# Middle layer norm of five chunks without a second transposition: centred B and a product on GpSimd with spread deviations

## The chip, the cores and the metric

One core of one Trainium2 chip runs the kernel. The metric is device time in microseconds, the median of three runs of the kernel before: 383.70 us (383.51 to 383.71). TensorE runs the matmuls and the transposes (PE in the profile, with its weight loads as PEld), VectorE (DVE) and ScalarE (ACT) work between them, GpSimd (POOL) does elementwise work in SBUF, and SyncE (SP) issues transfers.

## What is computed

The reference is a block of feed-forward, recurrent layer, feed-forward on an input of 8 sequences, 512 positions and 128 features, in float32:

```python
x = x + 0.5 * ffn(layernorm(x))      # ffn: silu(x W1) * (x W2), two gelu layers of 512, back to 128
z = layernorm(x)                     # the middle norm
xB = z @ B                           # B is 128 x 16
h_t = tanh(xB_t + h_(t-1) @ A.T)     # scan over 512 positions
x = x + (h @ C) @ W_out.T + b_out
x = x + 0.5 * ffn(layernorm(x))
```

layernorm takes mean and variance over the 128 features, without weights. Only `z @ B` is needed of the middle norm.

## The kernel before

The 4096 tokens are cut into 8 chunks of 512. The feed-forward network runs on one chunk after the other, 16 turns in all (8 chunks, two networks), with features on the partitions and 512 tokens along the free axis. Each large matmul is done twice, with a high and a low float32r part of its input (`y_hi`, `y_lo`), accumulated in one PSUM bank. ScalarE computes the activations and their rounded high parts; VectorE and GpSimd subtract to get the low parts. Each engine has its own hand-written order, and they meet only through semaphores that count up.

A turn g on TensorE is: layer 2 of chunk g (four output tiles m, four inputs k), with layer 4 of chunk g - 1 inside it, then layer 1 of chunk g + 1, layer 3 of chunk g. Turns 1 to 5 are `early_turn`; turns 3 to 5 also carry eight steps of the scan, and turns 4 and 5 are a hardware loop. In turn g the middle norm of chunk g - 1 (`mid`) is made. Its steps in the kernel before are:

- VectorE's `layer4` writes the chunk's residual stream to `x1c`; SP saves it.
- `middle_tokens` transposes `x1c` on TensorE, four 128 x 128 blocks into the bank `MI`: tokens on the partitions.
- `middle_stats` takes mean and variance on VectorE (`mv_m`), and `inverse_std("m", ...)` on GpSimd makes `rs_m`, the inverse deviations (128 x 4: token on the partition, block along the free axis).
- `normalise("m", ...)` on VectorE, four instructions, writes the normed tokens to `xnt_m`.
- `to_features("m", ...)` transposes them back on TensorE, four more blocks, line L316 of the profile.
- `middle_copy` on ScalarE copies them from `MI` to `xn2`.
- `x_times_b`, the last of TensorE's turn, multiplies `xn2` with `b_rep` (B twice over) into the bank `SC`, and `keep_xb` on ScalarE saves the result.

The first norm of the chunks 3 to 7 is done in another way already: GpSimd's `spread_std` writes mean and inverse deviation to `mr`, SP writes them to DRAM (`mr_row`) and reads them back as one row broadcast to all partitions (`mr_rep`, in the freed part of `w_raw`), and GpSimd's `spread_normalise` subtracts and multiplies, tokens along the free axis.

GpSimd's order in an early turn is: `spread_std`, `inverse_std("m")`, then `rest` (y2_lo of k = 0 and 2, y1_lo of k = 0 of the next chunk, y3_lo of k = 0, y1_lo of k = 1 and 2), then `spread_normalise`. The line L1507 is y1_lo, L1513 y2_lo or y3_lo. VectorE does the others: y2_lo and y3_lo on L853 and y1_lo of k = 3 on L848, behind the cast `y1_high` on L840. SP's loop over k = 0 to 4 is: `save_x1`, the write of `mr_row` (L1643), and its broadcast (L1646).

The scan's matrices are split and masked by `mix_parts` and `mix` on VectorE (L895, L899, L906). They stand in the turns that carry no scan step, which are the turns 1 and 2; both turns run them whole.

Of the kernel before, what the change touches and what calls it, by code (L numbers as in the profile page):

```python
# [48 lines left out]
WARM = 19  # L49
TURNED = 3  # L50
# [10 lines left out]
def build(nc, xT, xtok, w1T, w2T, h1T, h2T, w3T, scales, Ablk, Brep, CTrep, WoutT, ident_d, mask_d, outT):  # L61
    with ExitStack() as ctx:
# [52 lines left out]
        b_rep = sb("b_rep", [P, 2 * STATES])  # L115
        ct = sb("ct", [P, P])
# [106 lines left out]
        x1_saved = sem("x1_saved")  # L223
        xn2_r = sem("xn2_r")
# [42 lines left out]
        def through_t(kind, g):  # L267

            return turned(g) if kind == "f" else g
# [13 lines left out]
        def _(pe):  # L283
# [146 lines left out]
            def x_times_b(c):  # L430
                pe.wait_ge(xn2_r, c + 1)
                wait(pe, step_h, (c - SKIP) * CSTEPS)

                for j in range(2 * HALVES):
                    half = j % HALVES
                    mm = nc.tensor.matmul(SC[j * 2 * STATES:(j + 1) * 2 * STATES, 0:HCOLS], b_rep[:, :],  # L436
                                          xn2[:, half * HCOLS:(half + 1) * HCOLS], start=True, stop=True)
                mm.then_inc(xb_mm, 1)

# [22 lines left out]
            def early_turn(g, gen, mid, scan):  # L462
# [14 lines left out]
                layer2(g, 1, gen)  # L477
                middle_tokens(mid, 0)
# [8 lines left out]
                to_features("m", xnt_m, MI, mid)  # L487
# [9 lines left out]
                if isinstance(mid, int) and mid == 0:  # L497
                    pe.wait_ge(ld_scan, 48)
                x_times_b(mid)
# [273 lines left out]
        def _(dve):  # L773
# [34 lines left out]
            def normalise(kind, g, bankt, mv, rs, out):  # L808
                dve.wait_ge(rstd[kind], g + 1)
                wait(dve, feat[kind], through_t(kind, g))  # L810
                for q in range(QT):
# [43 lines left out]
            def layer4(phase, g, c):  # L855
                dve.wait_ge(l4_mm, g + 1)
                if phase == 0:
                    dve.wait_ge(ld_xall, 16)
                    wait(dve, x1_saved, 16 * g)
                    wait(dve, tok["m"], g)  # L860
                    res, dst = cols(x_all, c), x1c[:, :]
# [27 lines left out]
            def mix_parts(i):  # L889

                if i == 0:
# [4 lines left out]
                    return  # L896
                dve.wait_ge(ld_scan, 48)
# [31 lines left out]
            def early_turn(g, mid, scan):  # L929
                def step(t):  # L930
                    if scan is not None and t is not None:
                        scan_low(scan, t)
                    if scan is None and t in (0, 1):
                        mix_parts(t)
                    if scan is None and t == 6:
                        mix(0)
                    if scan is None and t == 7:
                        mix(1)
                        mix(2)
# [9 lines left out]
                normalise("m", mid, MI, mv_m, rs_m, xnt_m)  # L949
# [251 lines left out]
        def _(act):  # L1201
# [44 lines left out]
            def middle_copy(c):  # L1246
                act.wait_ge(feat["m"], c + 1)
# [28 lines left out]
            def early_turn(g, mid, scan):  # L1276
# [17 lines left out]
                middle_copy(mid)  # L1294
# [201 lines left out]
        def _(pool):  # L1496
            def inverse_std(kind, g, mv, ve, rs):
# [3 lines left out]
                wait(pool, normed[kind], through_t(kind, g))  # L1501
# [38 lines left out]
            def early_turn(g, mid):  # L1540
                spread_std(g + 2)
                inverse_std("m", mid, mv_m, ve_m, rs_m)
                rest(g, True)
# [14 lines left out]
            def rest(g, nxt):  # L1558
                low(g, 0, y2_hi_r, 2, y23, y2_hi, y2_lo, y2_lo_pool, (l3_mm, 4 * g))
                low(g, 2, y2_hi_r, 2, y23, y2_hi, y2_lo, y2_lo_pool, (l3_mm, 4 * g))  # L1560
# [162 lines left out]
```

## Time and profile before

| | |
|---|---|
| median of the runs | 383.70 us |
| the profiled execution: its time / its span | 383.75 us / 381.8 us |
| TensorE busy | 374.3 us, 98% of the span |
| VectorE / ScalarE / GpSimd busy | 74% / 68% / 47% |
| chain that ended last, TensorE's share | 92% |

The busy time of an engine says how full it is on the average, not which wait ends last. The chain follows the work back from the last instruction, each time to what released it. A timeline gives start, duration, engine, line, operation, output and inputs of each instruction, and in square brackets the idle time before it with the event that ended it. Starts are in microseconds from the span's start.

### The profile page before, as it was taken

The numbers are of one execution on the slowest core, as the hardware profiler recorded it, in microseconds if no ns is written. First come the engines' busy times: TensorE is split into PE (matmuls) and PEld (weight loads), VectorE is DVE, ScalarE is ACT, GpSimd is POOL, SyncE is SP. The second block draws the span as 40 slices with busy tenths as digits, with TensorE's granted clock in tenths as the row PEclk, the third lists the DMA queues.
The fourth block names the chain that finished last, engine by engine and source line by source line (L and its number), as shares of the span: only waits on it lengthen the run. The fifth ranks groups of instructions, "written<-read, shape, count | busy, mean of one in ns | idle before, by whom it ended". The sixth has DMA issues, their size and how long they took to land.

```text
span 381.8 us, 6521 instructions
## 1 busy us (share of the span) xinstructions
PE 374.3 (98%) x1773; PEld 297.2 (78%) x1773; DVE 283.3 (74%) x719; ACT 261.4 (68%) x605; POOL 177.8 (47%) x161
## 2 busy tenths in 40 slices
PE   7999999999999999999999999999999999999995
PEld 6877776867878787878778788888888788887774
DVE  5977989797797877677868866767867677686713
ACT  3889585676858678676685767858576875857654
POOL 2645264685646658342551623535324352533421
PEclk9999999999999999999999999999999999999999
DMA  7920010202001020000001000010100101010000
GB/s 225 433 116 1 28 57 15 70 2 83 3 29 55 2 83 0 27 1 29 28 2 55 3 28 27 2 55 2 56 0 15 40 0 55 0 40 17 2 28 32
DMA packets 7805, 16.64 MB, mean 44 GB/s; under 512 B 1888, under 2 KB 2912, under 8 KB 7520
## 3 DMA queue, kind: packets, MB, share of 16 engines
q1 hardware_dynamic: 6768, 16.01, 11.1%
q10 hardware_dynamic: 1008, 0.29, 0.3%
q8 instruction: 12, 0.20, 0.2%
q14 instruction: 17, 0.14, 0.1%
HBM read 9.99 MB, written 2.12 MB: 32 GB/s over the span
## 4 chain that ended last, share of the span: by engine, by line
PE 92%; DVE 4%; ACT 2%; issue 1%; DVEq 0%; ACTq 0%
PE F L288 71%; PE FR L288 8%; PE SC L504 2%; DVE y_lo L853 1%; PE FR L316 1%; PE F L541 1%; PE F L532 1%; ACT y_hi L1236 1%; DVE cw_mix L906 1%; PE MI L296 1%; PE MI L316 1%; PE FR L306 1%; PE SC L288 1%; PE SC L436 1%; PE F L534 1%
## 5 line engine op out<-in xcount | busy, mean ns | idle before, releaser
L288 PE MATMUL F<-y_hi,w_hi 128*128 128x512 f32 (+1 forms) x484 | 197.2, 408 | 0.9 <-DVE y_lo L853 0.6
L288 PE MATMUL F<-y_lo,w_hi 128*128 128x512 f32 (+1 forms) x484 | 188.4, 390 | 0.0
L288 PEld LDWEIGHTS F<-y_hi,w_hi 128*128 128x128 f32 x484 | 90.9, 188 | 25.4 <-issue 6.8
L1233 ACT ACTIVATE y<-F,sc 128x512 f32<-128x512 f32 x111 | 76.1, 686 | 43.5 <-PE F L288 42.3
L288 PEld LDWEIGHTS F<-y_lo,w_hi 128*128 128x128 f32 x484 | 91.2, 188 | 15.3
L1507 POOL TENSOR_TENSOR y_lo<-y,y_hi 128x512 fp32r<-128x512 f32 x48 | 66.7, 1396 | 59.0 <-DVE y_hi L840 48.1
L853 DVE TENSOR_TENSOR y_lo<-y,y_hi 128x512 fp32r<-128x512 f32 x79 | 64.9, 822 | 38.7 <-ACT y_hi L1236 38.7
L1513 POOL TENSOR_TENSOR y_lo<-y,y_hi 128x512 fp32r<-128x512 f32 x48 | 62.6, 1311 | 35.4 <-ACT y_hi L1236 35.4
L1236 ACT ACTIVATE y_hi<-F,sc 128x512 fp32r<-128x512 f32 x111 | 76.1, 685 | 0.0
L1252 ACT ACTIVATE h<-SC 128x32 fp32r<-128x32 f32 x96 | 18.8, 196 | 49.3 <-PE SC L451 48.3
L288 PE MATMUL F<-xn_hi,w_hi 128*128 128x512 f32 x118 | 49.4, 418 | 0.0
L823 DVE SCALAR_TENSOR_TENSOR u<-th,F 128x512 f32<-128x512 f32 x61 | 41.5, 680 | 8.1 <-ACT th L1215 8.0
L288 PE MATMUL F<-xn_lo,w_hi 128*128 128x512 f32 x118 | 46.2, 392 | 0.0
L833 DVE SCALAR_TENSOR_TENSOR y<-F,s12h,u 128x512 f32<-128x512 f32 x58 | 43.3, 747 | 1.6
L1215 ACT ACTIVATE th<-F,s1h 128x512 f32<-128x512 f32 x61 | 41.3, 689 | 2.5 <-PE F L288 2.5
L872 DVE TENSOR_TENSOR h<-SC,h 64x32 fp32r<-64x32 f32 x96 | 17.1, 178 | 18.3 <-ACT SC L1253 17.7
L1499 POOL TENSOR_TENSOR ve_f<-mv_f,epsc 128x4 f32<-128x4 f32 x11 | 2.2, 203 | 56.9 <-DVE mv_f L781 52.3
L288 PEld LDWEIGHTS F<-xn_hi,w_hi 128*128 128x128 f32 x118 | 22.1, 188 | 6.2 <-DVE y L833 0.6
L288 PEld LDWEIGHTS F<-xn_lo,w_hi 128*128 128x128 f32 x118 | 22.3, 189 | 3.5
L288 PE MATMUL FR<-y_hi,w_hi 128*128 128x512 f32 x60 | 24.0, 400 | 0.0
L288 PE MATMUL FR<-y_lo,w_hi 128*128 128x512 f32 x60 | 23.5, 391 | 0.0
L451 PEld LDWEIGHTS SC<-h,a_mix 128*128 128x128 f32 x95 | 17.8, 188 | 6.5 <-DVE h L872 2.8
(177 smaller groups left out, 443.8 us busy)
## 6 DMA issues: line engine op xcount, KB each, us to landing
w_raw<-mr_row SPq DMA_DIRECT2D x5, 512.0 KB, 3.4
x_all<-in_xT SPq DMA_DIRECT2D x1, 2048.0 KB, 16.5
x_all<-x1c SPq DMA_DIRECT2D x8, 256.0 KB, 2.3
x_all<-lnin SPq DMA_DIRECT2D x8, 256.0 KB, 2.2
out<-outb SPq DMA_DIRECT2D x7, 256.0 KB, 2.0
x_all<-in_xtok SPq DMA_DIRECT2D x1, 1536.0 KB, 12.2
w_raw<-in_h1T SPq DMA_DIRECT2D x2, 512.0 KB, 8.1
w_raw<-in_h2T SPq DMA_DIRECT2D x2, 512.0 KB, 9.6
```

The costliest lines, as they stand in the source:

```text
L288: mm = nc.tensor.matmul(out, wtile(w, layer, k, m), y, start=first and i == 0, stop=last and i == len(pairs) - 1)
L451: nc.tensor.matmul(SC[:, span(t)], a_mix[:, :], states, start=False, stop=True, skip_group_check=True).then_inc(step_mm, 1)
L823: nc.vector.scalar_tensor_tensor(out=u[:, m % 2, :], in0=th[:, m % 2, :], scalar=1.0, in1=l1_banks(g, m, late)[0][:, :], op0=ALU.add, op1= ...
L833: nc.vector.scalar_tensor_tensor(out=y1[:, m, :], in0=l1_banks(g, m, late)[1][:, :], scalar=s12h[:, m:m + 1], in1=u[:, m % 2, :], op0=ALU. ...
L853: nc.vector.tensor_tensor(y_lo[:, k, :], y[:, k, :], y_hi[:, k, :].bitcast(F32), ALU.subtract).then_inc(out_sem, 1)
L872: nc.vector.tensor_tensor(h[0:64, span(t)], SC[0:64, span(CSTEPS + t)], h[0:64, span(t)].bitcast(F32), ALU.subtract).then_inc(step_h, 1)
L1215: nc.scalar.activation(th[:, m % 2, :], l1_banks(g, m, late)[0][:, :], ACT.Tanh, scale=s1h[:, m:m + 1]).then_inc(th_r, 1)
L1233: nc.scalar.activation(y23[:, m, :], bankt[:, :], ACT.Gelu, scale=s)
L1236: nc.scalar.activation(y_hi[:, m, :], bankt[:, :], ACT.Gelu, scale=s).then_inc(hi_r, 1)
L1252: nc.scalar.activation(h[:, span(t)], SC[:, span(t)], ACT.Tanh)
L1507: pool.tensor_tensor(y1_lo[:, m, :], y1[:, m, :], y1_hi[:, m, :].bitcast(F32), ALU.subtract).then_inc(y1_lo_r if m < KT - 1 else y1_lo_las ...
L1513: pool.tensor_tensor(y_lo[:, k, :], y[:, k, :], y_hi[:, k, :].bitcast(F32), ALU.subtract).then_inc(out_sem, 1)
```

## The change

For the five chunks whose middle norm falls in the early turns, the norm is no longer applied to the tokens. The mean over the features is taken off B instead of x: TensorE multiplies B with a matrix that holds 1/128 everywhere (`b_mean`, once, in turn 1), and VectorE subtracts that from B (`b_cent`). Each token's inverse deviation is multiplied into `x1c`: SP writes `rs_m` to DRAM and broadcasts it as one row over the partitions (`rs_rep`), and GpSimd's `scale_x1` multiplies, reading that row with a step of four elements, into `xnt_m`, which `x_times_b` reads. The second transposition, `normalise("m")` and `middle_copy` go in these turns; the three later chunks keep them. `mix_parts` and the first `mix` stay in turn 1 only, and the second and third `mix` come in turn 2.

```diff
+SCALED = CHUNKS - FIRST
+        rs_row = nc.dram_tensor("rs_row", (P, QT), F32)
+        rs_rep = w_raw[:, 2 * N:3 * N]
...
-            def x_times_b(c):
-                pe.wait_ge(xn2_r, c + 1)
+            def x_times_b(c, scaled=False):
+                if scaled:
+                    pe.wait_ge(x1_scaled, c + 1)
+                    wait(pe, sc_set, c)
+                else:
+                    pe.wait_ge(xn2_r, c - SCALED + 1)
                 wait(pe, step_h, (c - SKIP) * CSTEPS)
+                b, src = (b_cent, xnt_m) if scaled else (b_rep, xn2)
...
+            def b_mean():
+                pe.wait_ge(ld_scan, 48)
+                pe.wait_ge(av_set, 1)
+                pe.wait_ge(u_r, 8)
+                nc.tensor.matmul(SC[:, 0:2 * STATES], averages[:, :], b_rep[:, :], start=True, stop=True).then_inc(b_mean_mm, 1)
...
                 layer2(g, 1, gen)
+                if isinstance(g, int) and g == 1:
+                    b_mean()
                 middle_tokens(mid, 0)
...
                 step(4)
-                to_features("m", xnt_m, MI, mid)
                 layer3(g, 0, gen)
...
-                x_times_b(mid)
+                x_times_b(mid, True)
...
                     wait(dve, tok["m"], g)
+                    wait(dve, x1_scaled, min(g, SCALED) if isinstance(g, int) else g)
...
+                dve.wait_ge(b_mean_mm, 1)
+                nc.vector.tensor_tensor(b_cent[:, :], b_rep[:, :], SC[:, 0:2 * STATES], ALU.subtract).then_inc(b_cent_r, 1)
...
-                    if scan is None and t in (0, 1):
+                    if isinstance(g, int) and g == 1 and t in (0, 1):
                         mix_parts(t)
-                    if scan is None and t == 6:
+                    if isinstance(g, int) and g == 1 and t == 6:
                         mix(0)
-                    if scan is None and t == 7:
-                        mix(1)
-                        mix(2)
+                    if isinstance(g, int) and g == 2 and t in (1, 2):
+                        mix(t)
...
-                normalise("m", mid, MI, mv_m, rs_m, xnt_m)
...
-                middle_copy(mid)
...
-                rest(g, True)
+                rest(g, True, lambda: scale_x1(mid))
                 spread_normalise(g + 2)
...
+            def scale_x1(c):
+                pool.wait_ge(l4_out, c + 1)
+                pool.wait_ge(rs_spread, 16 * (c + 1))
+                wait(pool, xb_mm, c)
+                pool.tensor_tensor(xnt_m.rearrange("n (q p) -> n q p", p=P), x1c.rearrange("n (q p) -> n q p", p=P),
+                                   rs_rep.rearrange("n (p q) -> n q p", q=QT), ALU.mult).then_inc(x1_scaled, 1)
+
+            def rest(g, nxt, between=lambda: None):
                 low(g, 0, y2_hi_r, 2, y23, y2_hi, y2_lo, y2_lo_pool, (l3_mm, 4 * g))
                 low(g, 2, y2_hi_r, 2, y23, y2_hi, y2_lo, y2_lo_pool, (l3_mm, 4 * g))
+                between()
                 if nxt:
                     layer1(g + 1, range(1))
...
                 sp.dma_start(mr_row[:, :], mr[:, :, :].rearrange("p q t -> p (q t)")).then_inc(mr_saved, 16)
+                sp.wait_ge(rstd["m"], k + 1)
+                sp.dma_start(rs_row[:, :], rs_m[:, :]).then_inc(rs_saved, 16)
+                sp.wait_ge(rs_saved, 16 * (k + 1))
+                wait(sp, x1_scaled, k)
+                sp.dma_start(rs_rep, rs_row.rearrange("p n -> (p n)").partition_broadcast(P)).then_inc(rs_spread, 16)
                 sp.wait_ge(mr_saved, 16 * (k + 1))
                 wait(sp, spread_normed, k)
```

## Rows read from the trace of the kernel before

**Rows 1.** Page, part 4: the chain that ended last, shares by engine.
```profile
PE 92%; DVE 4%; ACT 2%; issue 1%; DVEq 0%; ACTq 0%
```

**Rows 2.** TensorE's timeline, turn 4 and its end: start, duration, what.
```profile
118.13 0.64 PE L316 MATMUL MI<-ident,xnt_m 128*128 128x128 f32 x4
118.52 0.47 PE L288 MATMUL F<-y_hi,w_hi 128*128 128x512 f32 x1
...
131.83 0.39 PE L288 MATMUL F<-y_lo,w_hi 128*128 128x512 f32 x1
132.05 0.42 PE L288 MATMUL F<-y_hi,w_hi 128*128 128x512 f32 x1
```

**Rows 3.** TensorE's timeline at the seam of turns 1 and 2.
```profile
62.77 0.39 PE L288 MATMUL F<-y_lo,w_hi 128*128 128x512 f32 x1
63.45 0.47 PE L288 MATMUL F<-y_hi,w_hi 128*128 128x512 f32 x1 [0.29 <-DVE y_lo L853]
```

**Rows 4.** VectorE's timeline, end of turn 1.
```profile
57.56 2.69 DVE L906 SCALAR_TENSOR_TENSOR cw_mix<-part_lo,mask,part_own 128x128 fp32r<-128x128 f32 x2
...
62.62 0.69 DVE L853 TENSOR_TENSOR y_lo<-y,y_hi 128x512 fp32r<-128x512 f32 x1
```

**Rows 5.** GpSimd's timeline, turn 4: y1_lo(0), y3_lo(0), spread product.
```profile
121.35 1.29 POOL L1507 TENSOR_TENSOR y_lo<-y,y_hi 128x512 fp32r<-128x512 f32 x1 [3.14 <-DVE y_hi L840]
123.03 1.29 POOL L1513 TENSOR_TENSOR y_lo<-y,y_hi 128x512 fp32r<-128x512 f32 x1 [0.38 <-ACT y_hi L1236]
...
129.06 1.31 POOL L1532 TENSOR_TENSOR xnt_f<-xnt_f,w_raw 128x512 f32<-128x512 f32 x1
```

**Rows 6.** VectorE's timeline, turn 4.
```profile
115.73 1.37 DVE L812 TENSOR_SCALAR xnt_m<-MI,mv_m,rs_m 128x128 f32<-128x128 f32 x4 [0.78 <-POOL rs_m L1502]
...
120.77 0.42 DVE L840 CAST y_hi<-y 128x512 fp32r<-128x512 f32 x1
...
129.23 1.42 DVE L840 CAST y_hi<-y 128x512 fp32r<-128x512 f32 x1
130.58 0.68 DVE L853 TENSOR_TENSOR y_lo<-y,y_hi 128x512 fp32r<-128x512 f32 x1
131.18 0.68 DVE L848 TENSOR_TENSOR y_lo<-y,y_hi 128x512 fp32r<-128x512 f32 x1
```

**Rows 7.** ScalarE's timeline, turn 4: y3_hi(0).
```profile
122.27 0.68 ACT L1236 ACTIVATE y_hi<-F,sc 128x512 fp32r<-128x512 f32 x1
```

**Rows 8.** SP's timeline, turns 2 and 4: write and broadcast of the spread.
```profile
68.17 0.33 SPq L1643 DMA_DIRECT2D mr_row<-mr  x1
70.55 0.32 SPq L1646 DMA_DIRECT2D w_raw<-mr_row  x1
...
113.32 0.33 SPq L1643 DMA_DIRECT2D mr_row<-mr  x1
114.73 0.32 SPq L1646 DMA_DIRECT2D w_raw<-mr_row  x1
```

**Rows 9.** Page, part 6: transfers, KB each, median us from issue to landing.
```profile
w_raw<-mr_row SPq DMA_DIRECT2D x5, 512.0 KB, 3.4
...
x_all<-x1c SPq DMA_DIRECT2D x8, 256.0 KB, 2.3
```

**Rows 10.** Tile w_raw, 40 to 170 us: ns min/median/max of its GpSimd readers.
```profile
L1530 POOL TENSOR_TENSOR xnt_f<-x_all,w_raw x5: 1347/1749/1756, 58.8 to 150.0; 128x512 f32<-128x512 f32 x5
L1532 POOL TENSOR_TENSOR xnt_f<-xnt_f,w_raw x5: 1308/1323/1857, 60.2 to 151.8; 128x512 f32<-128x512 f32 x5
```

**Rows 11.** GpSimd's timeline, turns 1 and 2: rs_m and y3_lo(0).
```profile
46.68 1.06 POOL L1502 TENSOR_TENSOR rs_m<-ve_m,mhalf 128x4 f32<-128x4 f32 x1
...
54.49 1.30 POOL L1513 TENSOR_TENSOR y_lo<-y,y_hi 128x512 fp32r<-128x512 f32 x1 [0.33 <-ACT y_hi L1236]
...
68.74 1.07 POOL L1502 TENSOR_TENSOR rs_m<-ve_m,mhalf 128x4 f32<-128x4 f32 x1
...
77.11 1.30 POOL L1513 TENSOR_TENSOR y_lo<-y,y_hi 128x512 fp32r<-128x512 f32 x1 [0.55 <-ACT y_hi L1236]
```

## What I predict

> **What bounds the kernel now.** I read the chain of work that ended last first, then TensorE's timeline, then the timelines of the engines that feed it. The chain is TensorE for 92% of the span [rows 1], so a microsecond counts only if TensorE gets it. The chain's remainder says where TensorE is fed too late. TensorE's timeline shows how full it is: in the fourth early turn (106 to 129 us) one 512-column matmul starts 0.22 us after the other [rows 2], and over the five early turns only two places stand out, at the seams of turns 1 and 2 and of turns 2 and 3: there the next matmul starts 0.68 us after the one before and is released by VectorE's y_lo [rows 3]. That is 0.46 us of waiting; the second place looks the same.
>
> The reader should see next that TensorE's feed has no slack either. The last low part of a turn, y1_lo of k = 3, ends on VectorE at 131.86, and the matmul that needs it starts at 132.05, with nothing between [rows 2, 6]. What sets that end is GpSimd. VectorE's cast ahead of it takes 0.42 us at 120.77 and 1.42 us at 129.23 [rows 6]; the second stands over GpSimd's product, which ends at 130.37 [rows 5], and ends 0.28 us behind it. So VectorE's operations with only SBUF operands do not run beside a GpSimd operation: one of the two waits until the other has ended. From the start of y3_lo(0) on GpSimd (123.03) to the end of y3_lo(3) on VectorE (131.26) the two engines form one chain of 8.23 us [rows 5, 6]. In turn 1 the same chain is 54.49 to 63.31, 8.82 us [rows 11, 4]; the 0.59 us more are the mix instructions, two of which take 2.69 us while waiting for GpSimd [rows 4].
>
> **The change, part by part.** *Second transposition removed, five turns.* The four transposes start at 118.13 and the next matmul at 118.52 [rows 2]: 0.39 us of TensorE each turn, all on the path, 1.95 us in five turns. VectorE's four normalising instructions (1.37 us, begun after 0.78 us of waiting for rs_m) [rows 6] and ScalarE's copy go too; I cost both at nothing, since each engine next waits for a later event: VectorE for ScalarE's y2_hi, ScalarE for the next scan step. If that cover were gone nothing would get dearer, as this only takes work away.
>
> *Mean of B.* One 32-column float32 matmul, issued as two passes like the others of that type. A 128-column transposing matmul takes about 0.1 us (four in 0.39) [rows 2]; two passes cost 0.2 us, bounds 0.1 and 0.3. It is on the path of turn 1. The subtraction that centres B and the fill of the averages lie on VectorE and GpSimd beside TensorE's layer 2, at nothing.
>
> *Mix once.* Turn 2 loses its three mixes, turn 1 the last two, which go to the start of turn 2, where VectorE waits for GpSimd anyway. By chain length this is 0.59 us in turn 2; in turn 1 I leave a third of it in, so 0.4 us.
>
> *The product on GpSimd.* This is the new cost. It stands in GpSimd's queue after y2_lo(2) and ahead of y1_lo(0), and it waits for a broadcast. Behind it are y1_lo(0), y3_lo(0), y1_lo(1), y1_lo(2) and the two operations of the spread normalisation; TensorE waits for the low parts, ScalarE for the last. In the loop turn's clock: rs_m is there at 115.73, when its reader starts [rows 6]. SP writes it out; the same kind of write delayed the next issue by 1.41 us (113.32 to 114.73), once by 2.38 us (68.17 to 70.55) [rows 8]. Four turns of five show the short one, so 1.41: broadcast issued at 117.14. Its 256 KB lie between a small write (1.41 us) and the 512 KB broadcast (3.4 us), and other 256 KB transfers took 2.3 [rows 8, 9]; I take 2.4, bounds 2.3 and 3.4: landed at 119.54. The product's nearest rows are GpSimd's two operations with a strided second operand, 1.31 to 1.35 us undisturbed and 1.75 to 1.86 while waiting for VectorE [rows 10]. In the window of the product VectorE has only operations with a PSUM operand until the cast at 120.77, so I take 1.35, bounds 1.31 and 1.86. The product ends at 120.89.
>
> Then the cast waits 0.28 us past that end, y1_lo(0) starts 0.16 us after the cast (121.19 to 121.35) and takes 1.29 us [rows 5, 6]: y3_lo(0) can start 1.73 us after the product's end, at 122.62. Before it started at 123.03, released by ScalarE's y3_hi(0) [rows 5, 7]; with TensorE 0.39 us ahead that release comes at 122.64. So the product just fits: the saving of 0.39 us survives in turns 3, 4 and 5. Later ends cost one for one.
>
> *Turn 1.* rs_m ends at 47.74 [rows 11], 47.94 behind the mean of B. Plus 1.41, 2.4, 1.35 and 1.73 it is 54.83 for y3_lo(0), 0.34 us later than before [rows 11]. With a chain of 8.42 us (8.82 less 0.4) y3_lo(3) ends at 63.25 instead of 63.31: some 0.05 us gained, though TensorE alone would have had 0.39 + 0.46 - 0.2. *Turn 2.* rs_m ends at 69.81, y3_lo(0) could start at 76.70, released at 76.72 (77.11 less 0.39) [rows 11]; the chain is 0.59 us shorter, so TensorE gets all of its own: 0.39 + 0.46 = 0.85 us.
>
> *Order on SP.* The spread of the first norm's deviations (512 KB) is issued behind the new pair, some 2.8 us later, and shares the queue with it: by 3.4 us plus up to the new transfer's 2.4 it lands before 123.4. GpSimd reads it in the subtraction that stands one 1.75 us operation ahead of 129.06 [rows 5, 9, 10]: covered by about 3.9 us.
>
> **Sum.** Turn 1 0.05, turn 2 0.85, turns 3 to 5 three times 0.39: 2.07 us. The profiled execution took 383.75 us (span 381.8, 1.95 us around it), 0.05 us over the median of the runs. Forecast: 383.75 - 2.07 = 381.7 us.
>
> **A rule weighed against the trace.** The trace's rows with a second operand of 8-byte step are 1.31 to 1.35 us against 1.29 us for a contiguous one [rows 5, 10]: hardly dearer; the new product reads with a step of 16 bytes, which no row shows. The Trainium skill, "GPSIMD Engine Reference", section "7. Performance pitfalls for Q7 kernels", says that reads with a step over 8 bytes cost about one cycle more per element; an estimate from that page is 0.43 us more for 512 elements, and the sum by it would be about 383.7 us. No run here shows it yet.
>
> **The rivals.** *A: the strided read makes the product long.* Price: the longer rows of the same line, 1.75 us instead of 1.35 [rows 10]. The product then ends at 121.29 in the loop turn, y3_lo(0) starts at 123.02, and turns 3 to 5 gain nothing; turn 1 loses 0.35, turn 2 still gains about 0.6. The sum is -0.25: 383.5 us. For it: the step of 16 bytes has no row; against it: from 4 to 8 bytes almost nothing happened. *B, slower: the broadcast comes late and GpSimd's queue stands behind it.* Place: the wait ahead of the product. Price: each turn pays what the product ends later than figured, beyond the slack. With 3.4 us instead of 2.4 for the landing [rows 9]: turns 3 to 5 lose 0.6 each, turn 1 0.95, turn 2 nothing: +2.75, 386.5 us. It decides from 0.45 us of delay per turn, when the product ends after about 121.3 in the loop turn; 0.6 us make it slower by 0.2%. For it: one of five small writes took 2.38 us, and one engine's late packet is enough; against it: four of five agree within 0.03 us. Both ends together would be near 391 us, under 1 in 20. *C: the chain on GpSimd gives more than I read,* because VectorE's cast gets in ahead of the spread's product once the two drift apart: then TensorE's own savings all come through, 5 x 0.39 + 2 x 0.46 - 0.2 = 2.67: 381.1 us.
>
> **How the numbers follow.** Forecast 0.42 (381.3 to 382.8, its own range for the product ending up to 0.2 us later or a little earlier), A 0.27, B 0.21, C 0.10. The range takes in C and A whole and B as far as a delay of about 0.7 us per turn: 381.0 to 385.1, some 0.14 left out above and 0.04 below. A measurement of this kernel tells about 0.2% from no change. Faster by more: forecast and C, 0.52; within: A, 0.27; slower: B, 0.21.
>
> **What would show it.** Right: no transposes from xnt_m in turns 1 to 5; the seam waits of 0.68 gone or under 0.3 in turn 2; GpSimd's product starting 3.8 us after rs_m, lasting 1.35 us, and y1_lo(0) starting about 0.4 us behind it at most; turns 3 to 5 shorter by 0.39 us each. A is shown by a product of 1.7 us or more with y3_lo(0) not earlier in its turn than before; B by GpSimd idle on the broadcast past VectorE's cast, and by the cast stretched over the product. The sum fails if TensorE waits at the seams of turns 3 to 5 for y_lo, where it hardly did before.

## The result

The changed kernel takes 390.95 us in the median (390.0 to 391.62), the kernel before 383.51 us in the same comparison: a ratio of 1.0192 with an interval of 1.018 to 1.0205. It is slower by 7.4 us (1.9%), above the top of the forecast range (385.1). The profiled execution took 390.62 us, its span 389.0 us.

From the page of the kernel after: busy time of each engine (us, share of the span, instructions), the shares of the chain that ended last, and the transfers (KB each, median us from issue to landing).

```profile
PE 375.8 (97%) x1755; PEld 295.0 (76%) x1755; DVE 283.1 (73%) x692; ACT 258.9 (67%) x600; POOL 187.0 (48%) x167
...
PE 82%; DVE 7%; issue 5%; ACT 4%; POOL 0%; DVEq 0%; POOLq 0%
...
w_raw<-mr_row SPq DMA_DIRECT2D x5, 512.0 KB, 5.6
...
w_raw<-rs_row SPq DMA_DIRECT2D x5, 256.0 KB, 4.8
```

TensorE's share of the chain fell from 92% [rows 1] to 82%. The new broadcast, figured at 2.4 us, lands after 4.8 us, and the 512 KB one after 5.6 instead of 3.4 [rows 9].

The fourth turn shows what follows. First SP's own queue and GpSimd's timeline of the kernel after (start, duration, what; in brackets the idle time before it and what ended it).

```profile
120.00 0.32 SPq L1682 DMA_DIRECT2D rs_row<-rs_m  x1
121.41 0.32 SPq L1685 DMA_DIRECT2D w_raw<-rs_row  x1
121.83 0.37 SPq L1688 DMA_DIRECT2D w_raw<-mr_row  x1
```

```profile
118.97 1.01 POOL L1530 TENSOR_TENSOR rs_m<-ve_m,mhalf 128x4 f32<-128x4 f32 x1 [0.17 <-POOL ve_m L1524]
119.94 2.55 POOL L1541 TENSOR_TENSOR y_lo<-y,y_hi 128x512 fp32r<-128x512 f32 x2
126.52 1.56 POOL L1590 TENSOR_TENSOR xnt_m<-x1c,w_raw 128x512 f32<-128x512 f32 x1 [4.03 <-DMA w_raw<-rs_row]
128.05 1.28 POOL L1535 TENSOR_TENSOR y_lo<-y,y_hi 128x512 fp32r<-128x512 f32 x1
129.30 1.74 POOL L1541 TENSOR_TENSOR y_lo<-y,y_hi 128x512 fp32r<-128x512 f32 x1
```

rs_m ends at 119.98, its write delays the next issue by 1.41 us as figured, the broadcast is issued at 121.41, and the product starts at 126.52, after 4.03 us in which GpSimd does nothing. That is 6.54 us after rs_m instead of 3.8. y1_lo(0) and y3_lo(0) stand behind it. VectorE's cast for y1_lo(0) had been done at 125.47, a microsecond before the product began. So GpSimd is idle on the broadcast past the cast, the first of the two signs that were named for rival B; the second, a cast stretched over the product, did not come. The end of the turn comes late:

```profile
125.05 0.42 DVE L865 CAST y_hi<-y 128x512 fp32r<-128x512 f32 x1
...
134.24 1.29 DVE L865 CAST y_hi<-y 128x512 fp32r<-128x512 f32 x1
135.45 1.79 DVE L878 TENSOR_TENSOR y_lo<-y,y_hi 128x512 fp32r<-128x512 f32 x1
```

```profile
135.78 0.40 PE L299 MATMUL F<-y_lo,w_hi 128*128 128x512 f32 x1
137.30 0.50 PE L299 MATMUL F<-y_hi,w_hi 128*128 128x512 f32 x1 [1.12 <-DVE y_lo L878]
```

Above is VectorE, below TensorE at the seam of turns 4 and 5, where the kernel before had no wait [rows 2]. There are 1.52 us between two starts instead of 0.22. The five seams after turns 1 to 5 show 1.40, 1.40, 1.24, 1.52 and 1.56 us; before, the first two had 0.68 and 0.67 [rows 3], the others nothing. Less the usual 0.22 us each, that is 6.0 us of waiting instead of 0.9.

A table made from the starts of `x_times_b`, the last work of TensorE's turn, shows every turn and serves the experiments too. An interval n to n + 1 holds the seam behind turn n and the transposes of turn n + 1 (turn 6 keeps its own).

| us | start in turn 1 | 1 to 2 | 2 to 3 | 3 to 4 | 4 to 5 | 5 to 6 | product after rs_m, turn 4 |
|---|---|---|---|---|---|---|---|
| before | 59.41 | 22.62 | 23.49 | 22.65 | 22.75 | 14.49 | - |
| after | 59.93 | 24.25 | 24.35 | 23.81 | 24.33 | 16.17 | 6.5 |
| e1, spread first | 59.89 | 25.15 | 24.75 | 24.69 | 24.39 | 16.55 | 6.6 |
| e2, spread behind | 59.56 | 24.35 | 23.57 | 23.61 | 23.24 | 15.47 | 5.4 |
| e5, old row | 59.93 | 24.13 | 22.51 | 22.45 | 22.41 | 14.53 | 3.2 |
| e6, own rows | 60.18 | 24.30 | 22.53 | 22.42 | 22.44 | 14.53 | 2.8 |
| e3, one broadcast | 59.34 | 24.87 | 22.55 | 22.40 | 22.41 | 14.52 | 2.5 |
| e4, mix once alone | 59.34 | 22.44 | 22.86 | 22.65 | 22.63 | 14.51 | - |
| e11, the same again | 59.24 | 22.11 | 22.89 | 22.64 | 22.75 | 14.51 | - |
| e7, contiguous | 59.21 | 24.12 | 24.23 | 24.00 | 23.77 | 15.82 | 6.3 |
| e8, VectorE scales, slow write | 59.89 | 22.41 | 22.62 | 22.86 | 22.63 | 15.07 | - |
| e9, row in pieces | 59.90 | 22.45 | 22.65 | 22.86 | 22.61 | 14.54 | - |
| e10, and mix later | 59.84 | 22.13 | 22.59 | 22.87 | 22.59 | 14.53 | - |

After minus before: 0.52 up to turn 1's end, then 1.63, 0.86, 1.16, 1.58 and 1.68, together 7.4 us. So the whole difference lies in the turns that the change touches, and most of it (5.1 us) at their seams.

Each row is one execution. e4 and e11 are the same kernel and differ by 0.33 us in the interval 1 to 2 and by at most 0.12 in the others. The first column also holds what ran before turn 1, where kernels with the same code differ: GpSimd's first step of turn 1 (`ve_f`) starts anywhere from 44.11 (e7) to 45.07 us (e6). From that step to `x_times_b`, turn 1 lasts 14.61 us before and 14.63 and 14.60 in e4 and e11, 15.09 to 15.13 in the kernels with the change, and 14.79 in e10.

### The profile page after: what moved, and what is told of

The parts are those of the page before. It is cut to its first block, busy times and chain, and to the rows that moved or that the text cites. A ratio compares the mean times of both kernels' runs of the same rounds, so it can differ in the third digit from the quotient of the medians.

```text
span 389.0 us, 6478 instructions
## 1 busy us (share of the span) xinstructions
PE 375.8 (97%) x1755; PEld 295.0 (76%) x1755; DVE 283.1 (73%) x692; ACT 258.9 (67%) x600; POOL 187.0 (48%) x167
## 4 chain that ended last, share of the span: by engine, by line
PE 82%; DVE 7%; issue 5%; ACT 4%; POOL 0%; DVEq 0%; POOLq 0%
PE F L299 63%; PE FR L299 7%; DVE y_lo L878 2%; ACT y_hi L1262 2%; PE SC L527 2%; PE FR L327 1%; PE F L564 1%; DVE y L858 1%; DVE u L848 1%; PE F L555 1%; ACT y L1259 1%; PE MI L307 1%; PE FR L317 1%; PE SC L299 1%; DVE y_lo L873 1%
## 5 line engine op out<-in xcount | busy, mean ns | idle before, releaser
L878 DVE TENSOR_TENSOR y_lo<-y,y_hi 128x512 fp32r<-128x512 f32 x79 | 73.9, 935 | 42.4 <-ACT y_hi L1262 42.3
L1535 POOL TENSOR_TENSOR y_lo<-y,y_hi 128x512 fp32r<-128x512 f32 x48 | 67.5, 1414 | 43.9 <-DVE y_hi L865 33.2
L1541 POOL TENSOR_TENSOR y_lo<-y,y_hi 128x512 fp32r<-128x512 f32 x48 | 63.9, 1339 | 32.7 <-ACT y_hi L1262 32.7
L299 PEld LDWEIGHTS F<-xn_lo,w_hi 128*128 128x128 f32 x118 | 22.3, 189 | 3.4
```

The costliest lines, as they stand in the source:

```text
L299: mm = nc.tensor.matmul(out, wtile(w, layer, k, m), y, start=first and i == 0, stop=last and i == len(pairs) - 1)
L878: nc.vector.tensor_tensor(y_lo[:, k, :], y[:, k, :], y_hi[:, k, :].bitcast(F32), ALU.subtract).then_inc(out_sem, 1)
L1535: pool.tensor_tensor(y1_lo[:, m, :], y1[:, m, :], y1_hi[:, m, :].bitcast(F32), ALU.subtract).then_inc(y1_lo_r if m < KT - 1 else y1_lo_las ...
L1541: pool.tensor_tensor(y_lo[:, k, :], y[:, k, :], y_hi[:, k, :].bitcast(F32), ALU.subtract).then_inc(out_sem, 1)
```

## The experiments

The theory after the result was rival B: the broadcast lands late and GpSimd's queue waits behind it. What had to be told apart was why it lands late (S: it shares the transfer engines with the 512 KB broadcast issued 0.42 us behind it; W: it is slow by itself), whether the other savings are there at all when the wait is gone, and what each of the other parts is worth. Edits are shown shortened; words behind # in e3 and e6 are mine.

**e1: the order on SP turned round.** The 512 KB broadcast is issued ahead of the write and the broadcast of rs_m.

```diff
                 sp.dma_start(mr_row[:, :], mr[:, :, :].rearrange("p q t -> p (q t)")).then_inc(mr_saved, 16)
+                sp.wait_ge(mr_saved, 16 * (k + 1))
+                wait(sp, spread_normed, k)
+                sp.dma_start(mr_flat, mr_row.rearrange("p n -> (p n)").partition_broadcast(P)).then_inc(mr_spread, 16)
                 sp.wait_ge(rstd["m"], k + 1)
                 sp.dma_start(rs_row[:, :], rs_m[:, :]).then_inc(rs_saved, 16)
```

> The changed kernel with one order on SP turned round: the first norm's row and its 512 KB broadcast are issued first, as in the kernel before, and the new row and its 256 KB broadcast behind them. Theory S (the new broadcast is slow because the 512 KB one is issued 0.42 us behind it and shares the 16 DMA engines): the new broadcast lands in 2.4 to 3.0 us instead of about 5.1, its small row may wait behind the large broadcast's packets, the product starts 4 to 5 us after rs_m instead of 6.55, and the time is 382.5 to 386. Theory W (128 reads of one freshly written 2 KB row are slow by themselves): the product still starts 6 us or more after rs_m, and the time stays at 390 to 391.

Measured: 393.37 us, ratio 1.0263 (1.0238 to 1.0288); this is slower than the changed kernel, and above the range of both theories. From its transfers:

```profile
w_raw<-mr_row SPq DMA_DIRECT2D x5, 512.0 KB, 3.7
w_raw<-rs_row SPq DMA_DIRECT2D x5, 256.0 KB, 3.8
...
rs_row<-rs_m SPq DMA_DIRECT2D x5, 2.0 KB, 2.8
```

The 512 KB broadcast is fast again and the new one lands in 3.8, but now the small write takes 2.8 us instead of 1.4 behind the large transfer, and the product starts 6.6 us after rs_m. What is saved at one transfer is lost at the other. The expectation of S failed: with this order rs_m's data come as late as they did, or later.

**e2: the spread behind.** SP waits for the new broadcast before it issues the 512 KB one, so nothing of SP's runs beside it.

```diff
                 sp.dma_start(rs_rep, rs_row.rearrange("p n -> (p n)").partition_broadcast(P)).then_inc(rs_spread, 16)
+                sp.wait_ge(rs_spread, 16 * (k + 1))
                 sp.wait_ge(mr_saved, 16 * (k + 1))
```

> The changed kernel with one wait more on SP: the 512 KB broadcast is issued only when the new 256 KB one has landed. Theory S: the new broadcast, alone on the engines, lands in about 2.4 us, the product starts 3.9 us after rs_m, ends some 0.3 us late for turns 3 to 5 because it takes 1.56 us, and the time is 382 to 383.5; the large broadcast lands some 3 us later than in the changed kernel and is still early. Theory W: the new broadcast takes 4.5 us or more also alone, 390 to 391.

Measured: 388.35 us, ratio 1.0137 (1.0115 to 1.0158). It lies between the two expectations. Transfers, and SP's and GpSimd's timelines in the fourth turn:

```profile
w_raw<-mr_row SPq DMA_DIRECT2D x5, 512.0 KB, 3.6
w_raw<-rs_row SPq DMA_DIRECT2D x5, 256.0 KB, 3.9
```

```profile
120.18 0.32 SPq L1685 DMA_DIRECT2D w_raw<-rs_row  x1
124.11 0.32 SPq L1689 DMA_DIRECT2D w_raw<-mr_row  x1
```

```profile
124.17 1.56 POOL L1590 TENSOR_TENSOR xnt_m<-x1c,w_raw 128x512 f32<-128x512 f32 x1 [2.91 <-DMA w_raw<-rs_row]
```

So the sharing costs 0.9 us of landing (4.8 to 3.9), and the rest is the transfer's own: with no other transfer of SP's beside it, 256 KB took 3.9 us, more than the 3.6 of 512 KB. The product still comes 5.4 us after rs_m.

One turn of this run tells more. In the third the write is a long one, and SP issues the broadcast 2.50 us after it instead of 1.41:

```profile
95.28 0.32 SPq L1682 DMA_DIRECT2D rs_row<-rs_m  x1
97.78 0.32 SPq L1685 DMA_DIRECT2D w_raw<-rs_row  x1
100.89 0.32 SPq L1689 DMA_DIRECT2D w_raw<-mr_row  x1
```

SP issues the 512 KB transfer when the broadcast has landed, after 3.11 us here and 3.9 to 4.5 us in the other four turns. What the write took more, the broadcast took less: from the write's issue to the landing it is 5.6 us here, and 5.3 to 5.9 in the others.

**e3: no broadcast in the loop.** The rows are written and spread in turn 1 only; later turns multiply by those.

```diff
-            with sp.Fori(0, SPREAD) as k:
+            for k in range(1):        # whole, then without rs_row and rs_rep:
...
+            with sp.Fori(1, SPREAD) as k:
...
-                pool.wait_ge(rs_spread, 16 * (c + 1))
+                pool.wait_ge(rs_spread, 16)
```

> The changed kernel with the row of deviations broadcast in turn 1 only; the products of turns 2 to 5 multiply by the deviations of the first chunk, so the result is not the norm of those chunks. Turn 1 is as in the changed kernel, where it costs about 2.5 us up to the seam. If the wait for the broadcast is what costs (theories S and W alike): turns 2 to 5 get their products in GpSimd's idle time and gain 0.85 and three times 0.39 us: 383.2 to 384.8. If it is the product itself on GpSimd's queue (rival: 1.56 us more work on a full engine), turns 2 to 5 lose about as much as now: 388 or more.

Measured: 384.22 us, ratio 1.0026 (1.0013 to 1.004), as expected. The table is worth more than the total: with no wait, the intervals 2 to 3, 3 to 4 and 4 to 5 are 0.94, 0.25 and 0.34 us shorter than before, and 1 to 2, with the seam behind turn 1, which still has its broadcast, is 2.25 us longer. The seams behind turns 2 to 5 show no wait. So the savings exist, and what eats them is the wait for the broadcast.

**e5: an old row.** e2 with the row written in turn 1 only, and broadcast from DRAM again each turn: the same transfer of 256 KB from one row of 2 KB, but the row is not fresh.

```diff
+            with sp.Fori(1, SPREAD) as k:
...
                 sp.wait_ge(rstd["m"], k + 1)
-                sp.dma_start(rs_row[:, :], rs_m[:, :]).then_inc(rs_saved, 16)
-                sp.wait_ge(rs_saved, 16 * (k + 1))
                 wait(sp, x1_scaled, k)
                 sp.dma_start(rs_rep, rs_row.rearrange("p n -> (p n)").partition_broadcast(P)).then_inc(rs_spread, 16)
                 sp.wait_ge(rs_spread, 16 * (k + 1))
```

> As the run with the 512 KB broadcast behind the new one, but the row of deviations is written to DRAM in turn 1 only; turns 2 to 5 broadcast that old row again (so the norm of those chunks uses the first chunk's deviations), 1.4 us earlier because no write stands ahead. Where the new broadcast alone took 3.9 to 4.5 us from issue to landing, theory F (the row has only just been written, in pieces of 16 bytes) expects 2.3 to 3.0 us for the old row in turns 2 to 5; theory R (128 partitions read the same 2 KB) expects 3.5 us or more, unchanged. Either way the product starts 1.4 to 3 us earlier than with the fresh row, and the time falls from 388.4 to 384 to 386.

Measured: 383.37 us, ratio 1.0006 (0.9991 to 1.0021). Its transfer and the product of the fourth turn:

```profile
w_raw<-rs_row SPq DMA_DIRECT2D x5, 256.0 KB, 3.1
```

```profile
119.84 1.56 POOL L1590 TENSOR_TENSOR xnt_m<-x1c,w_raw 128x512 f32<-128x512 f32 x1 [0.66 <-DMA w_raw<-rs_row]
```

The same transfer lands 0.8 us sooner when its row has not just been written. The old row lies in DRAM as the fresh one does, written in 128 pieces of 16 bytes, so the pieces by themselves do not make the delay; the third turn of e2, where a fresh row landed in 3.1 us behind a long write, says the same. What passes between a write and a broadcast close behind it stays open, and the 512 KB broadcast shows no such delay: 3.4 us before, 1.4 us behind its row's write [rows 8, 9], and 3.6 in e2, where in the fourth turn its row was 7.7 us old. The product starts 3.2 us after rs_m, lasts the same 1.56 us, and the turns are as short as without any broadcast: a wait of 0.66 us on GpSimd costs nothing.

**e6: own rows.** As e5, but each partition reads back its own 2 KB from a DRAM copy of 256 KB, not 128 times the one row.

```diff
+                sp.dma_start(rs_full[:, :], rs_rep).then_inc(rs_kept, 16)     # turn 1
...
-                sp.dma_start(rs_rep, rs_row.rearrange("p n -> (p n)").partition_broadcast(P)).then_inc(rs_spread, 16)
+                sp.dma_start(rs_rep, rs_full[:, :]).then_inc(rs_spread, 16)   # turns 2 to 5
```

> As the run with the old row, but turn 1 also keeps the 256 KB as they lie in SBUF, and turns 2 to 5 read them back from DRAM, each partition its own 2 KB (so again the first chunk's deviations). Theory R (one row read 128 times) expects 2.3 to 2.6 us from issue to landing, as other 256 KB transfers take; theory F expects the same as for the old row. If the old row already lands in 2.3 to 3.0, this adds nothing; if the old row takes 3.5 or more and this one 2.5, R is shown.

Measured: 383.6 us, ratio 0.9999 (0.9984 to 1.0013).

```profile
w_raw<-rs_full SPq DMA_DIRECT2D x4, 256.0 KB, 2.6
```

It lands in 2.6 us, near the 2.3 us of the 256 KB transfers that I had gone by [rows 9]. Reading one row 128 times costs 0.5 us more. The turns gain nothing over e5, since there the wait was off the path already.

**e4: the matrices prepared once, and nothing else.** The kernel before with this part of the change alone.

```diff
-                    if scan is None and t in (0, 1):
+                    if isinstance(g, int) and g == 1 and t in (0, 1):
                         mix_parts(t)
-                    if scan is None and t == 6:
+                    if isinstance(g, int) and g == 1 and t == 6:
                         mix(0)
-                    if scan is None and t == 7:
-                        mix(1)
-                        mix(2)
+                    if isinstance(g, int) and g == 2 and t in (1, 2):
+                        mix(t)
```

> The kernel before with the scan's matrices prepared once, the one part of the change alone. By the prediction: the wait at the seam of turns 2 and 3 goes (0.46 us) and the one of turns 1 and 2 goes in good part (0.3 to 0.46): 382.6 to 382.9. Rival: GpSimd's chain holds the seams anyway, and nothing is gained: 383.3 to 383.7.

Measured: 382.27 us, ratio 0.9978 (0.9966 to 0.999): 0.8 us less than the kernel before beside it (383.04). That is the gain expected; the range in us was reckoned from a kernel before of 383.5, and the time lies below it. TensorE at the seam of turns 1 and 2, where rows 3 stood:

```profile
62.54 0.39 PE L288 MATMUL F<-y_lo,w_hi 128*128 128x512 f32 x1
62.83 0.47 PE L288 MATMUL F<-y_hi,w_hi 128*128 128x512 f32 x1
```

The wait is gone: 0.29 us between the starts instead of 0.68.

**e7: a contiguous second operand.** The changed kernel with the product reading the spread row without a step.

```diff
-                                   rs_rep.rearrange("n (p q) -> n q p", q=QT), ALU.mult).then_inc(x1_scaled, 1)
+                                   rs_rep.rearrange("n (q p) -> n q p", p=P), ALU.mult).then_inc(x1_scaled, 1)
```

> The changed kernel with the product's second operand read in the order in which it lies in SBUF (step of 4 bytes instead of 16; each token so gets another token's deviation). It prices the step: the product took 1.56 us. If the step costs, 1.29 to 1.35 us and a time lower by up to five times 0.25 us, 389.7 to 390.5; if not, 1.56 us and no change, 390.95.

The products of the kernel after, and those of this one (ns, least, median and most):

```profile
L1590 POOL TENSOR_TENSOR xnt_m<-x1c,w_raw x5: 1560/1562/1580, 54.8 to 150.6; 128x512 f32<-128x512 f32 x5
```

```profile
L1590 POOL TENSOR_TENSOR xnt_m<-x1c,w_raw x5: 1297/1302/1302, 54.2 to 149.3; 128x512 f32<-128x512 f32 x5
```

The step of 16 bytes costs 0.26 us. With these values the kernel runs further rounds of the scan behind the turns (480 steps instead of 96), so its whole time, 1652.9 us, tells nothing; its early turns can be compared. The last four intervals together are 87.82 us instead of 88.66: 0.21 us a turn come back from a product that is 0.26 shorter. So the length of the product counts nearly in full once the turns wait for it, but it is a small part of the 1.69 us that each of them lost (see below).

**e8: another place for the multiplication.** The idea was a version that keeps the savings: TensorE multiplies `x1c` by the centred B at once, and VectorE multiplies the 128 x 256 result by the deviations, about 13 us after rs_m, so that the row has time. GpSimd has no product. The row was written in single elements, so that it could be read without a step.

```diff
+            def scale_xb(c):
+                dve.wait_ge(xb_mm, c + 1)
+                dve.wait_ge(rs_spread, 64 * (c + 1))
+                nc.vector.tensor_tensor(SC[:, 0:HCOLS], SC[:, 0:HCOLS], rs_rep, ALU.mult).then_inc(xb_scaled, 1)
...
-                sp.dma_start(rs_row[:, :], rs_m[:, :]).then_inc(rs_saved, 16)
+                sp.dma_start(rs_row.rearrange("q p -> p q"), rs_m[:, :], allow_slow_non_contiguous=True).then_inc(rs_saved, 16)
```

> A version that follows from the runs so far: the deviations multiply the product with B (VectorE, 128 x 256, in the bank SC, between its last gate and the cast of a turn) and not x1 before it, so nothing on GpSimd waits for the broadcast, which is needed only at the end of the turn, some 10 us after its issue. No second transposition, no product on GpSimd, matrices prepared once. If the late broadcast in GpSimd's queue is what made the change slow, TensorE's savings all come through: 0.77 (matrices) and five times 0.25 to 0.39 less 0.2 for the mean of B and some 0.4 for turn 1: 380.5 to 382 at 383.0 for the kernel before. Rival: VectorE's extra operation at the seam costs 0.3 to 0.4 us each turn there: 382.5 to 384.

Measured: 383.67 us, ratio 1.0004 (0.9989 to 1.002). The expectation failed; the time lies in the range of its rival. Its transfer and VectorE at the seam:

```profile
rs_row<-rs_m SPq DMA_DIRECT2D x5, 2.0 KB, 9.1
```

```profile
106.19 0.43 DVE L954 TENSOR_TENSOR SC<-SC,w_raw 128x256 f32<-128x256 f32 x1 [0.26 <-DMA w_raw<-rs_row]
```

512 single elements of 4 bytes took 9.1 us to write. The write stands behind the 512 KB broadcast here; the same 2 KB in 128 pieces of 16 bytes take 2.7 us in that place (e9) and 1.4 us with nothing ahead (after). With 2.9 us for the spread behind it that uses up nearly all of the 13 us, and in two of the turns VectorE waits, 0.26 and 1.26 us. That is not the main loss, though: e9 has no such wait, and only its last interval is shorter (14.54 instead of 15.07).

**e9 and e10: the row in pieces, and the matrices later.** e9 is e8 with the row written in 16-byte pieces and read with a step; e10 is e9 with VectorE's second part of the matrices behind a later low part of turn 1. e11 is e4 once more, on the same chip.

```diff
-                sp.dma_start(rs_row.rearrange("q p -> p q"), rs_m[:, :], allow_slow_non_contiguous=True).then_inc(rs_saved, 16)
+                sp.dma_start(rs_row[:, :], rs_m[:, :]).then_inc(rs_saved, 16)
...
-                    if isinstance(g, int) and g == 1 and t in (0, 1):
+                    if isinstance(g, int) and g == 1 and t in (0, 2):
                         mix_parts(t)
```

> The kernel that scales the product of x and B by the deviations on VectorE, with the row written as in the changed kernel, 128 pieces of 16 bytes, and spread by four transfers of 32 partitions. Theory (what was left of the gain went into the row's slow write, 9.1 us, and the wait on VectorE behind it): the row is there 1.4 us after rs_m, the copies 4 to 5 us later, some 5 us ahead of VectorE's need, so no wait is left in any turn. Loops of 22.3 to 22.4 us instead of 22.4 to 22.9: 381.5 to 382.5 us beside 383.5 for the kernel before. Rival: VectorE's additional operation of 0.43 us a turn itself eats the transposes' time at the seam: 382.7 to 383.6, no better than the matrices prepared once alone.

> As the one with the row in pieces, with VectorE's second part of the matrices of turn 1 one step later, so that GpSimd's small power for rs_m does not meet VectorE's operations on SBUF. Theory (the power took 1.72 instead of 1.06 us because the two engines shut each other out): 1.06 again, turn 1 shorter by 0.3 to 0.5 us, 381.2 to 382.1 in all. Rival: the power is long for another reason, or the operations meet another one of GpSimd's: no difference to the run beside it, within 0.3 us.

> The kernel before with the matrices prepared once and nothing else, on the same chip as the two others, for comparison: 382.3 to 382.8 us as before (0.7 to 1.1 us under the kernel before). If the two others are under it by more than 0.4 us, the transposes' time has come through; if not, it has not.

Measured beside one kernel before of 383.44 us: e9 382.41 (ratio 0.9972, 0.9961 to 0.9982), e10 382.18 (0.9958, 0.9942 to 0.9973), e11 382.22 (0.9974, 0.9961 to 0.9986). All three are faster than before, by 0.3 to 0.4%, and no interval lies apart from another: the transposes' time has not come through as a gain that can be measured. e9 is inside its own range (381.5 to 382.5) only by what the matrices bring, and the turns of 22.3 to 22.4 us that it named did not come. In e9 VectorE waits no more for the row, but its operation takes longer, and a new wait appears on TensorE in the fourth turn:

```profile
L954 DVE TENSOR_TENSOR SC<-SC,w_raw x5: 610/612/617, 61.2 to 151.4; 128x256 f32<-128x256 f32 x5
```

```profile
119.56 0.18 PE L473 MATMUL SC<-h,a_mix 128*128 128x32 f32 x1
120.13 0.50 PE L299 MATMUL F<-xn_hi,w_hi 128*128 128x512 f32 x1 [0.39 <-DVE y L858]
```

TensorE now waits 0.39 us for VectorE's y, which empties its bank, and the interval 3 to 4 is 0.22 us longer than in e11, while 2 to 3 and 4 to 5 are 0.24 and 0.14 shorter. In the second turn it waits for the same event, 0.52 us:

```profile
74.84 0.50 PE L299 MATMUL F<-xn_hi,w_hi 128*128 128x512 f32 x1 [0.52 <-DVE y L858]
```

Here the time of the transposes can be followed. Counted from the `x_times_b` before, TensorE in e9 is 0.40, 0.36, 0.34 and 0.37 us ahead of e11 just behind the place where they stood in turns 2 to 5. At the next matmul that needs VectorE's y it is 0.24 behind in turn 2, 0.29 ahead in turn 3, 0.19 behind in turn 4 and 0.14 ahead in turn 5. So TensorE saves the time, and in turns 2 and 4 it loses more than that at its next wait. In turn 2 the reason can be read, VectorE and GpSimd of e9:

```profile
72.04 1.37 DVE L878 TENSOR_TENSOR y_lo<-y,y_hi 128x512 fp32r<-128x512 f32 x1 [2.57 <-ACT y_hi L1269]
```

```profile
70.31 2.54 POOL L1548 TENSOR_TENSOR y_lo<-y,y_hi 128x512 fp32r<-128x512 f32 x2
```

VectorE's y_lo takes 1.37 us instead of 0.68, since GpSimd's pair runs until 72.85, and y comes behind it. In turn 4 VectorE is idle for 0.41 us ahead of its y (119.33), and the profile names no event that ended this; why it comes late there, and in turn 5 in part, stays open.

GpSimd's power (the operation that makes rs_m) in e9 and in e10 is as the theory for e10 expected:

```profile
46.93 1.72 POOL L1537 TENSOR_TENSOR rs_m<-ve_m,mhalf 128x4 f32<-128x4 f32 x1
```

```profile
47.45 1.03 POOL L1537 TENSOR_TENSOR rs_m<-ve_m,mhalf 128x4 f32<-128x4 f32 x1
```

Turn 1, counted from `ve_f`, is 14.79 us in e10 and 15.09 in e9, the 0.3 us that were expected. The interval 1 to 2 fell too, from 22.45 to 22.13, but e4 and e11 differ there by as much. The times of the two kernels are 0.2 us apart, inside the 0.3 of the rival. The simplest kernel that beats both given ones is e4, by 0.2 to 0.3%: three conditions changed, 382.2 to 382.3 us.

## Why the prediction was wrong, point by point

**The step that failed: the landing of the broadcast.** I put it at 2.4 us with bounds of 2.3 and 3.4, between a small write and the 512 KB broadcast, and by size. It took 4.8. The runs split the excess: 2.6 us for 256 KB where each partition reads its own row (e6), 0.5 more for one row read 128 times (e5), 0.8 more when that row was written just before (e2), 0.9 more with the 512 KB transfer issued 0.42 us behind (after): 2.6 + 0.5 + 0.8 + 0.9 = 4.8. The upper bound was wrong in kind. The 512 KB broadcast was taken as the larger case of the same thing, but e2 shows the smaller one slower, 3.9 us against 3.6, with no other transfer of SP's beside it.

**The step that was half made: the order on SP.** I wrote that the 512 KB transfer "shares the queue with" the new one, and priced only what that does to the first, which had 3.9 us to spare. It slows the second too, which had nothing to spare: the 0.9 us of e2. The Trainium skill, "DMA: Bandwidth & Descriptors", section "Issuing engines are not separate DMA queues", says that all transfers end on the same 16 engines and interleave there; 5.6 us instead of 3.4 for the one and 4.8 instead of 3.9 for the other agree.

**The break-even came later than figured.** From the prediction follow two points. When the product ends more than 5.2 us after rs_m (120.89 less 115.70), a later end costs turns 3 to 5 one for one; from 5.59 us (121.29 less 115.70) on, nothing is gained any more over the kernel before. The last four intervals of the table show the first point. e5, e6 and e3 are alike (81.90, 81.92 and 81.88 us together), though the product starts 3.2, 2.8 and about 2.5 us after rs_m: below the point, nothing changes. e2, with 5.55 us in the mean of these turns, needs 85.89, so 1.00 more a turn; the kernel after, with 6.29, needs 88.66, 1.69 more a turn. From 0.74 us of delay 0.69 come back, nearly one for one, and the line meets zero at a start of 4.5, an end of 6.0 us after rs_m. Two runs that the line was not drawn from lie on it: by it e1, with a product that ends 8.37 us after rs_m, loses 2.17 us a turn, and 2.12 are measured; e7, with 7.63, loses 1.48, and 1.48 are measured.

So the point lies 0.8 us later than I figured, and two rows give the reason. The cast no longer stands between product and y1_lo(0), since it is done earlier, so y3_lo(0) starts 1.22 us behind the product's end (128.08 to 129.30), not 1.73. The chain behind it is 129.30 to 137.24, 7.94 us, where I read 8.23 [rows 5, 6]. With a write of 1.41 and a product of 1.56 us, an end at 6.0 leaves about 3.0 us for the landing. 4.8 is 1.8 too much, and the turns lost 1.69.

**The row's write** was right: 1.41 us in the fourth turn, and one of five was again long (the broadcast of turn 3 issued 2.32 us after rs_m). That one cost nothing, as in e2: its broadcast landed 3.6 us later, and the product of turn 3 starts 5.91 us after rs_m, the earliest of the five. Write and broadcast should have been priced together.

**The product** was put at 1.35 us and took 1.56. Rival A's mechanism is real with 0.26 us, two thirds of its price of 0.4; it did not decide, since e5 keeps every saving with a product of 1.56. The Trainium skill, "GPSIMD Engine Reference", section "7. Performance pitfalls for Q7 kernels", from which I had worked out an estimate of 0.43 us, has the sign right and the size too large for this operation of two inputs.

**The transposes** were put at 0.39 us a turn. Where the broadcast is out of the way (e3), TensorE is 0.37 and 0.41 us ahead behind their place in turns 4 and 5, and 0.25 and 0.34 us come through in the intervals 3 to 4 and 4 to 5. In turn 2 a wait for VectorE's y takes it back (0.52 or 0.53 us in e3, e5, e6 and e9). I had costed VectorE's part of this "at nothing"; that TensorE, coming earlier, would meet VectorE's y was not in the sum, nor in rival C's. In turn 1 nothing of it shows: from `ve_f` to `x_times_b` the kernel after is 0.52 us longer.

**The mean of B** was put at 0.2 us and shows as 0.19: the first 512-column matmul behind it starts at 44.92, before at 44.73. What I missed in turn 1 is GpSimd's power for rs_m, 1.72 us instead of 1.06 [rows 11]. GpSimd's y2_lo come later by it, and TensorE waits for one:

```profile
50.04 0.47 PE L299 MATMUL F<-y_hi,w_hi 128*128 128x512 f32 x1 [0.30 <-POOL y_lo L1541]
```

The spacing there is 0.69 us, in e10 0.33. I had costed the work on VectorE in turn 1 "at nothing". e10, where VectorE's operations stand in another order, shows a power of 1.03 us, so the order matters; which operation makes the power long is not shown. In the kernel after `part_own` and y_lo stand beside it. But before, y_lo ran beside it (first line; the power from 46.68 to 47.74), and in e10 `part_own` does (second line; the power from 47.45 to 48.48), and neither is stretched:

```profile
46.80 0.68 DVE L853 TENSOR_TENSOR y_lo<-y,y_hi 128x512 fp32r<-128x512 f32 x1
```

```profile
47.34 0.67 DVE L927 TENSOR_SCALAR part_own<-part_hi,mask 128x128 f32<-128x128 f32 x3
```

So the prediction's sentence that VectorE's operations with only SBUF operands do not run beside a GpSimd operation is too wide: it fits the cast and the product of 512 columns [rows 5, 6], and not these.

**The matrices prepared once** were right in mechanism and in size: I gave them 0.4 us in turn 1 and the seam wait of 0.46 in turn 2, 0.9 together, and alone they bring 0.8 us (e4) and, by its ratio, 1.0 (e11).

**The chances.** What came is rival B, to which I gave 0.21, with both extremes together "near 391 us" and under 1 in 20. That 391 was measured is chance: the figure was to come from a landing of 3.4 us and a long write in every turn, and what came was a short write in four turns and a landing of 4.8. The profile spoke for it more than I let it: the whole slack was 0.45 us, and the row that carried it, the landing, was the one with no near neighbour in the trace.

## What to carry to other kernels

A value that goes over DRAM to be spread over the partitions needs its real landing time, of the same pattern (fresh, small pieces, one row for all), not one by size; if the trace has none, the upper bound is above the largest neighbour. When a transfer is put beside another on the same engines, price what each does to the other, and ask first for the one with a waiting reader. And when a change has several parts, run the cheap one alone: here three conditions brought all of the gain that could be measured. Time taken off the busiest engine is worth only what its next wait leaves of it: follow the saving to that wait before it is added up.

## What the runs showed of the hardware

- The landing of 256 KB into 128 partitions depends on the pattern more than on the size: 2.6, 3.1, 3.9 and 4.8 us for own rows, one old row, one fresh row, and one fresh row beside another broadcast. A fresh row whose write took 1.1 us longer landed in 3.1 (e2, turn 3).
- 2 KB written to DRAM behind a broadcast of 512 KB took 9.1 us in single elements of 4 bytes (e8) and 2.7 in pieces of 16 bytes (e9). The Trainium skill, "DMA: Bandwidth & Descriptors", section "Specifications", names 512 bytes as the least for line rate; both are far below it, and between them lies a factor of more than three. With nothing ahead, the 16-byte pieces took 1.4 us (after).
- A small write queued behind a broadcast of 512 KB took 2.8 us (e1) and 2.7 (e9) instead of 1.4.
- VectorE's subtraction of 512 columns took 1.37 instead of 0.68 us beside two of GpSimd's (e9, turn 2), and ended 0.56 us behind them. The Trainium skill, "SBUF — State Buffer", section "🔬 SBUF: two separate sides", describes the two engines' shared ports as an exclusive lock; this row agrees, but in turn 1 of the kernel before a subtraction of the same form ran its 0.68 us inside GpSimd's operation on 128 x 4 elements. That small operation took 1.72 us in the kernel after and 1.03 in e10, by the order of VectorE's operations around it.
- A second operand with a step of 16 bytes cost 0.26 us on GpSimd (512 elements, 1.30 to 1.56) and 0.18 us on VectorE with the other operand in PSUM (256 elements, 0.43 to 0.61).
